# Values projected by pair of groups, and the streams of steps placed anew in one hand-written order

## The reference, cut to what matters

```
xn1 = layernorm(x) * g1 + be1
q, k, v = xn1 @ Wq + bq, xn1 @ Wk + bk, xn1 @ Wv + bv      # per head, 32 wide
scores = (q @ k^T) / scale, masked with -inf above the diagonal
sa  = softmax(scores) @ v
x   = x + sa @ W1 + b1
```

## Time and profile before

| | us |
|---|---|
| median of 3 executions | 2349.78 (2348.75 to 2349.86) |
| span of the profiled execution, first to last instruction | 2338.9 |
| PE busy | 2198.0 (94%) |
| DVE busy | 1410.1 (60%) |
| POOL busy | 933.6 (40%) |
| ACT busy | 868.2 (37%) |
| start of unit 0 / unit 4 / unit 8 / unit 12 | 113.3 / 344.0 / 570.4 / 798.8 |
| start of unit 14 / unit 15 | 898.7 / 965.4 |

### The profile page before, as it was taken

One profiled execution on the slowest core, in us unless ns is written; L12 is line 12 of the kernel. 1 busy time (PEld: TensorE's weight loads), 2 busy tenths in 40 slices (PEclk: granted clock), 3 DMA queues, 4 the chain that ended last, 5 costly groups with the idle time before them and its releaser, 6 DMA issues.

```text
span 2338.9 us, 31417 instructions
## 1 busy us (share of the span) xinstructions
PE 2198.0 (94%) x11206; PEld 1595.5 (68%) x11206; DVE 1410.1 (60%) x3349; ACT 868.2 (37%) x1598; POOL 933.6 (40%) x943
## 2 busy tenths in 40 slices
PE   7999999999999998789999998999999999999996
PEld 5655565556555654447777776788887887888784
DVE  5477757875786566735666668453455546454646
ACT  3155545654565455533443334321111122112213
POOL 1068657766777577773333333010111202011212
PEclk9999999999999998789999999999999999999998
DMA  7465545553556356212111121321112121212011
GB/s 231 55 93 97 92 71 77 103 93 62 83 97 97 60 88 124 69 56 85 59 55 55 59 95 55 113 86 36 50 54 75 52 82 44 87 55 68 33 36 50
DMA packets 106320, 177.29 MB, mean 76 GB/s; under 512 B 18334, under 2 KB 23454, under 8 KB 106160
## 3 DMA queue, kind: packets, MB, share of 16 engines
q1 hardware_dynamic: 106164, 175.29, 32.4%
HBM read 83.67 MB, written 40.13 MB: 53 GB/s over the span
## 4 chain that ended last, share of the span: by engine, by line
PE 75%; DVE 9%; issue 6%; ACT 4%; POOL 3%; DMA 2%; SPq 0%; POOLq 0%; ACTq 0%; DVEq 0%
PE psum L55 18%; PE psum L56 17%; PE psum L57 17%; PE psum L797 5%; PE psum L745 5%; PE psum L785 4%; PE psum L806 2%; DMA small<-es 2%; PE psum L703 1%; DVE psum L1000 1%; POOL es L660 1%; ACT sx L1346 1%; PE psum L1300 1%; DVE mx L1004 1%; PE psum L1292 1%
## 5 line engine op out<-in xcount | busy, mean ns | idle before, releaser
L660 POOL TENSOR_TENSOR es<-es,er 128x512 f32<-128x512 f32 (+3 forms) x640 | 589.6, 961 | 322.5 <-PE psum L797 283.4
L895 ACT ACTIVATE er<-psum 128x512 f32<-128x512 f32 (+3 forms) x640 | 280.4, 470 | 316.0 <-DVE psum L1011 181.2
L1000 DVE CUSTOM_DVE_ANT_0 psum<-psum,mask_ts 128x384 f32<-128x384 f32 (+3 forms) x512 | 247.9, 500 | 201.2 <-PE psum L745 200.5
L785 PE MATMUL psum<-qs,ks 100*128 100x512 f32 (+3 forms) x768 | 264.5, 377 | 17.1 <-DVE mx L1004 6.6
L745 PE MATMUL psum<-ks,qs 96*128 96x512 f32 (+3 forms) x768 | 267.2, 373 | 10.9 <-DVE mx L1000 6.6
L1850 ACT ACTIVATE fy<-psum,cols 128x512 f32<-128x512 f32 x128 | 88.2, 689 | 451.4 <-PE psum L57 450.9
L745 PEld LDWEIGHTS psum<-ks,qs 96*128 96x128 f32 x768 | 144.0, 194 | 109.7 <-issue 39.4
L1004 DVE TENSOR_REDUCE mx<-psum 128x1 fp32r<-128x512 f32 x256 | 175.1, 684 | 60.7 <-PE psum L745 59.8
L785 PEld LDWEIGHTS psum<-qs,ks 100*128 100x128 f32 x768 | 145.9, 196 | 92.4 <-DVE mx L1004 23.1
L55 PE MATMUL psum<-fh,hh 128*128 128x512 f32 x512 | 201.1, 393 | 7.1 <-DVE hl L1951 7.1
L55 PE MATMUL psum<-fah,fh 128*128 128x512 f32 x512 | 202.6, 396 | 0.0
(11 more groups left out here) (258 smaller groups left out, 4479.8 us busy)
## 6 DMA issues: line engine op xcount, KB each, us to landing
qs<-stage SPq DMA_DIRECT2D x96, 256.0 KB, 5.7
ks<-stage SPq DMA_DIRECT2D x96, 256.0 KB, 6.9
rs<-rs_d SPq DMA_DIRECT2D x32, 256.0 KB
sa_d<-rs SPq DMA_DIRECT2D x32, 256.0 KB, 2.2
sx<-sa_d SPq DMA_DIRECT2D x8, 1024.0 KB, 5.7
xt<-in_x SPq DMA_DIRECT2D x32, 256.0 KB, 6.1
x_d<-xt SPq DMA_DIRECT2D x32, 256.0 KB, 2.0
fw<-in_Wf SPq DMA_DIRECT2D x16, 512.0 KB, 5.3
```

The costliest lines, as they stand in the source:

```text
L660: e.tensor_tensor(es, es, er, ALU.add).then_inc(s_add.sem, 1)
L785: t = e.matmul(ps[:, off:512], Q.ks[par][0:100, i, 128 * j:128 * j + 128], Q.qs[par][0:100, i, 512 * c2 + off:512 * c2 + 512], start=True, ...
L895: e.activation(dst, bank1("sc", g, c2, j, i)[:, off:512], ACT.Exp, scale=SCALE).then_inc(s_freeS.sem, 1)
L1000: t = e.tensor_tensor_reduce(out=ps, in0=ps, in1=mask_ts[:, 512 - wd:512], scale=1.0, scalar=-3e38, op0=ALU.add, op1=ALU.max, accum_out=mx ...
```

## The change

1. **Values by pair of groups.** The 8 steps of 512 columns per batch element become 8 steps over two *pairs* q = g // 2 (256 of the 512 columns each): 4 steps `sp` per pair, each of two 128-token blocks. A step has 4 parts, each of 2 k-tiles, so 24 matmuls of 256 columns instead of 12 of 512. One bank and one `ve` (ACT, 512 columns) per step, as before.
2. **`Q.v` becomes a double buffer by pair** (`values(g)`: half g // 2 % 2 of the same memory). `ve` of pair q waits for the last `pv` of group 2q-3, the pair before the last, and for the first two pairs for the `lnT` that read the rows of `x` which lie there at the start.
3. **Positions.** `cut` and the positions of projections, values, row maxima and the normalization now depend on g % 4. Values of the even pair (group g = 4b) stand at g - 1.149, - 0.992, - 0.719, - 0.081; those of the odd pair (group 4b + 2) at g - 1.444, - 1.08, - 0.796, - 0.377. Of group 0 and 1 the maxima are moved ahead.
4. **Cross-attention set-up.** Every position of its first steps is changed a little, the split of `W2` from 15.08 to 15.576, that of `Wq_c` from 14.74 to 14.853, that of `W1` from 14.4 to 14.581; X0 from 16.68 to 16.793.

```
+LN_LOAD = (-2.514, -2.024, -1.712, -1.56)
+LN_TURN = (-2.071, -1.822, -1.573, -1.348)
+CUT = (0.292, 0.27, 0.283, 0.294)
+PROJ_0 = (27.2, 31.3, 37.9, 40.4)
+PROJ_1 = (-1.329, -1.236, -1.109, -1.047)
+PROJ = ((-1.661, -1.491, -1.269, -1.082), (-1.853, -1.456, -1.346, -1.171), (-1.872, -1.647, -1.316, -1.202), (-1.958, -1.475, -1.34, -1.21))
+PROJ_LONG = (0.067, 0.08, 0.146, 0.146)
+VALUES_0 = (40.2, 52.3, 66.7, 68.9)
+VALUES = ((-1.149, -0.992, -0.719, -0.081), (-1.444, -1.08, -0.796, -0.377))
+VALUES_LONG = 0.1
+MAX_0 = -0.007
+MAX_1 = (-0.809, -0.507, -0.024)
+MAX = ((-1.031, -0.726, -0.051), (-1.012, -0.739, -0.002), (-1.033, -0.705, -0.043), (-0.988, -0.72, -0.05))
...
-    cut = 0.31
...
-                t += ln_times(b, qt, 4 * b - 2.5 if qt == 0 else 4 * b - 2.28 + 0.26 * qt, 4 * b - 2.05 + 0.25 * qt)
...
-                s, d = 4 * b - 1 + cut + (1 - cut) * (st + 2.2) / 9, 0.057
+            t += ln_times(b, qt, 4 * b + LN_LOAD[qt], 4 * b + LN_TURN[qt])
...
-        elif g % 4 == 0:
-            at = (g - 1.67, g - 1.5, g - 1.22, g - 1.11)
-        else:
-            at = (max(g - 1.87, 0.2), max(g - 1.63, 0.4), g - 1.4, g - 1.2)
+        at = [at0(a) for a in PROJ_0] if g == 0 else [g + a for a in (PROJ_1 if g == 1 else PROJ[r])]
+        if g % 2 == 0:
+            for sp in range(4):
+                s, d = (at0(VALUES_0[sp]), 0.05) if g == 0 else (g + VALUES[r // 2][sp], VALUES_LONG)
+                t += spread(s, s + d, [(("vm", g // 2, sp, i), 1) for i in range(4)])
+                t.append((s + d, ("ve", g // 2, sp)))
...
-    T, X0 = 0.207, 16.68
+    T, X0 = 0.207, CROSS_AT
-        for j, at in enumerate((14.4, 14.74, 15.08)):
+        for j, at in enumerate(CROSS_SPLIT):
...
+        def values(g):
+            return Q.v[:, 4 * (g // 2 % 2):4 * (g // 2 % 2) + 4, :].rearrange("p a (s n) -> p (a s) n", n=256)
...
-                    t = three(e, bank1(*s[:3]), (Q.xh[:, k, ss], Q.xl[:, k, ss]), (Wh[:, k, :], Wl[:, k, :]), k == 0, k == 3)
+                    for k in range(2 * (i % 2), 2 * (i % 2) + 2):
+                        t = three(e, bank1(*s[:3])[:, to], (Q.xh[:, k, ss], Q.xl[:, k, ss]), (Wh[:, k, cs], Wl[:, k, cs]), k == 0, k == 3)
...
-                    if b:
-                        w.wait_ge(s_pv, Q.pv[4 * b - 1, 1, st, 3] + 1)
+                    if q >= 2:
+                        w.wait_ge(s_pv, Q.pv[2 * q - 3, 1, 2 * sp + 1, 3] + 1)
+                    else:
+                        w.wait_ge(s_fillA, Q.useA["lnT", 0, 2 * q + sp // 2, 1] + 1)
```

More of the change, by code:

```diff
@@ L142, in order1 @@
             t.append((at0(at + 4), ("zo", u)))
[L143 removed]
+    for b in range(1, NB):
         for qt in range(4):
[L145 to L162 removed]
+            t += ln_times(b, qt, 4 * b + LN_LOAD[qt], 4 * b + LN_TURN[qt])
+    for g in range(16):
+        r = g % 4
+        cut = CUT[r]
+        at = [at0(a) for a in PROJ_0] if g == 0 else [g + a for a in (PROJ_1 if g == 1 else PROJ[r])]
         for c2 in range(2):
@@ L165, in order1 @@
                 n = 2 * c2 + wq
[L166 to L169, removed]
+                t += proj_times(g, c2, wq, at[n], at[n] + (0.05 if g < 2 else PROJ_LONG[r]))
@@ new lines, in order1 @@
+                back = g - 2 + (CUT[(g - 2) % 4] if n == 0 else CUT[(g - 2) % 4] + (1 - CUT[(g - 2) % 4]) * 0.54 if n == 1 else 1) + 0.03
+                t.append((at[n] + 0.1 if g == 0 else max(at[n] + PROJ_LONG[r] + 0.07, back), ("stack", g, c2, wq)))
+        if g % 2 == 0:
[3 more added lines that the diff above has]
+                t.append((s + d, ("ve", g // 2, sp)))
@@ L170, in order1 @@
+        m0, m1, end = (at0(46), at0(54), MAX_0) if g == 0 else [g + a for a in (MAX_1 if g == 1 else MAX[r])]
         t += spread(m0, m1, max_steps(g, 0)) + spread(m1, end, max_steps(g, 1))
-        for c2, at in enumerate((m1, end)):
-            t += [(at + 0.04, ("mxT", g, c2)), (at + 0.06, ("tq", g, c2)), (at + 0.09, ("tqd", g, c2))]
+        for c2, a in enumerate((m1, end)):
+            t += [(a + 0.04, ("mxT", g, c2)), (a + 0.06, ("tq", g, c2)), (a + 0.09, ("tqd", g, c2))]
         for c2 in range(2):
-            steps = spread(g + cut * c2, g + (1 if c2 else cut), attn_steps(g, c2))
+            end = g + (1 if c2 else cut)
+            steps = spread(g + cut * c2, end, attn_steps(g, c2))
@@ L175, in order1 @@
             t += steps
-            for at, s in steps:
-                if s[0] == "sc" and s[3] >= 4 * c2:
-                    t += [(at + 0.014, ("low", *s[1:])), (at + 0.028, ("ex", *s[1:]))]
+            for a, s in steps:
+                if s[0] == "sc" and s[3] >= 4 * c2 :
+                    t += [(a + 0.014, ("low", *s[1:])), (a + 0.028, ("ex", *s[1:]))]
                 elif s[0] == "sc":
-                    t.append((at + 0.001, ("ex", *s[1:])))
-            end = g + (1 if c2 else cut)
+                    t.append((a + 0.001, ("ex", *s[1:])))
@@ L240, in order2 @@
         if c == 0:
-            ld, sp, w1, step, ln = 15.78, 15.86, 15.9, 0.07, 16.22
+            (ld, sp, w1, ln), step = CROSS_0, 0.07
         else:
@@ L484, in released @@
             elif use[0] == "vm":
-                w.wait_ge(s_v, 8 * use[1] + use[2] + 1)
+                w.wait_ge(s_v, 4 * use[1] + use[2] + 1)
             elif use[0] == "pj":
```

47 lines of the change are left out of this document (27 added, 20 removed).

## The result

| | before | after |
|---|---|---|
| median | 2349.27 us (4 runs) | 2276.62 us (2275.13 to 2281.93, 4 runs) |
| ratio | | 0.9708, 95% interval 0.9694 to 0.9723 |
| span of the profiled execution | 2338.9 us | 2280.1 us |

The changed kernel is 72.7 us faster; 26 were forecast, and the result lies 20 us under the low end of the range (2297). In this and all sixteen later profiled kernels the execution's own time is known, and it is 1.77 to 1.84 us above the span. So the "10.9 us outside the span" of the prediction was no fixed part: by the same 1.8 us the profiled execution of before took about 2340.7 us, 9 under its median (its own time is not known), and that of after took 2281.93, 5 over its own. The spans therefore show 59 of the 73 us; the other 14 are scatter between executions.

What follows compares the result with a forecast made beforehand. PE, busy 94% of the span, was taken as the bound, so time is won only where it idles or does less work. Terms 2.9 - 14 - 3 - 7 - 3 - 2 = -26 gave 2324 us, range 2297 to 2356.

Steps and rivals of the forecast that it cites:

- 256 columns: Value matmuls on PE: 768 of 256 columns replace 384 of 512, 0.12 us apart; +2.9 us, bounds 0 and +57.
- Rival D: Value matmuls on PE: the weight load sets the pace of 256 columns at 0.19 us; 2378 us, chance 2%.
- Values spread, -14: Attention units: value steps, spread from lumps of 7 and 1, cover PE's waits; -14 us, bounds -28 and +7.
- Double buffer at nothing: `ve` on ACT waits for groups ending over 0.6 of a unit earlier; counted as nothing.
- Projections, maxima, normalization at -3: Small position shifts: POOL stands up to 1.7 us more at `rs`, against better `CUT` shares; -1 per batch element, -3.
- Unit 14 at -7: Unit 14: moved splits shrink the 9.73 us DVE instruction to 1 to 3 us; -7 us, bounds -17 and +17.
- Hand-over at -3: PE's waits entering the next stage: attention's last steps move behind the first wait; -3 us, bounds -11 and +9.
- Clock at -2: Units 5 to 7: value steps nearby remove one or two clock dips of 1.7 us; -2 us, bounds -5 and +3.
- Span to median: Before the first and behind the last instruction: median 10.9 us above the 2338.9 us span, taken as unchanged.
- A: Whole kernel: no change worth the name, steps land where PE is busy anyhow; 2350 us, chance 19%.
- B: Units, normalization, unit 14 and hand-over: all holes filled; 2294 us, chance 15%.
- C: DVE's splits at new places are caught by POOL's adds, up to 8.7 us each; 2360 us with three, chance 12%.

Runs made afterwards that it cites:

- values_only: Changed kernel with every position but the values' set back to those of the kernel before; -34.8 us against the kernel before.
- w1_pool_q_late: Changed kernel with the low part of `W1` made by POOL instead of DVE and the `Wq_c` split at 15.28; 2277.3 us.
- best: `w1_pool_q_late` with the projections of groups 0 and 1 ahead of unit 0 at their old positions; 2274.7 us.
- old_cross: Changed kernel with all positions of the cross-attention's first steps as before; costs 11 us against the changed kernel.
- its control: The changed kernel itself run once more, on the same chip as other experiments; -71.3 us against the kernel before.
- old_ln0: Changed kernel with the normalization and the projections of each batch element's first group at their old positions; 2300.2 us.
- old_lnproj: Changed kernel with normalization and all projections at their old positions; 2320.6 us.
- late_pv: Kernel before with the last `pv` of each half 0.03 of a unit later and its result's copy 0.02 later; 2342.6 us.
- splits_late: Changed kernel with the `W1`, `Wq_c` and `W2` splits later (14.86, 15.28, 15.6) and `W2`'s load at 15.07; 2276.7 us.
- old_max: Changed kernel with the row maxima at their old positions, also those of groups 0 and 1; 2283.6 us.

## Why the prediction was wrong

**The bound on PE.** Right: the time was won in PE's gaps, and the kernel got faster.

**256 columns.** Right: 0.12 us apart, a step at 2.85 to 2.88 us where 2.79 were, some +2 to +3 us in all. Rival D is out. By an estimate from the Trainium skill ("TensorE: Matmul & The Clock Gate", Back-to-back issue gap), whose figures for a stream are 81 ns at 128 columns and 131 ns at 512, two matmuls of 256 would have cost more than one of 512 by at least 31 ns; this trace has 0.24 against 0.233 us, so the row decides.

**Values spread, -14, bounded by -28. This step failed.** It subtracted the value steps from units 4 and 7 and took the remainder, 47.5 us, as what a unit needs. The remainder is the least that was *seen*; units 4 and 7 still lost 7.2 and 7.8 us of it. After the change the same remainder is 45.0 to 45.5 in every unit from 3 to 13 without the normalization's last three quarters, and in `values_only` it is 44.8 to 45.7 in units 7, 11 and 13. The 2.3 us between, times 14 units, are 32 us, and the stretch ahead of unit 14 was forecast to lose 16 us and lost 49. The expected lengths were off by these 2.3 us and by the 0.7 to 1.0 us that the working held back as not covered: 54 for units 5, 9 and 13, measured 50.8, 50.9, 50.7; 57 for units 7 and 11, measured 54.1; unit 4 to unit 8 222, measured 211.0. Net of value steps and transposes, units 4 to 7 became shorter by 1.9, 7.0, 5.0 and 2.3 us, where 0, 2.5, 2.0 and -0.4 were counted; six maxima left unit 5, so part of its 7.0 only moved. By itself the spread gave -35 (`values_only`), beyond its own lower bound.

**Double buffer at nothing.** Not measured by itself; it is a condition of the spread.

**Projections, maxima, normalization at -3. Failed too.** The working looked at one queue, POOL at `rs`, and expected it to stand longer; in unit 6 it stands 2.65 us in place of 5.55, and over the kernel 46.9 in place of 48.8. It also took the new `CUT` as nearer to the first half's real share of a unit, "16.5 of 50". That share is 0.33, and the new 0.27 to 0.29 are farther from it than the old 0.31; in the long units 6 and 7 the same 16 us are 0.27 and 0.25. Set back one at a time, all but the first two groups' projections (0) cost more than the whole term: normalization and first projections 24, other projections 13, `CUT` 24, maxima 7. These costs and the values' 50 are far more than 72 together: they are not shares of the gain. I read each as what it costs when one stream no longer fits the others; by which wait it does stays open. The same new normalization and projections without their partners gave -0.5.

**Unit 14 at -7.** Wrong in place and mechanism. The stall stayed (9.78 us; expected under 4), unit 14 was 64.1 and 60.2 us (expected under 61), and the kernels without the stall (`w1_pool_q_late`, `best`) were no faster. One `Wq_c` split of 4.10 us was caught as well.

**Hand-over at -3.** Measured -5.3 in the traces. The trace of `old_cross` is 5.5 us ahead of the changed kernel's at unit 15's start and loses 9.2 behind it; the two medians are 11 apart.

**Clock at -2.** Half-clock time fell from 27.3 to 6.8 us in the profiles, at most -10; kernels with nearly the same order had 0 to 13.7. In the changed kernel and its control all of it lies in unit 2, in `old_ln0` in units 2, 6 and 10 (6.8 us each), so it adds to what is lost where the normalization runs; in `old_lnproj` unit 0 has 13.7 of the 41.0 us. In the kernel before it was spread over units 1, 2, 6, 9 and 10.

**Span to median.** The 10.9 us "outside the span" are 1.8; that put 9 us of scatter into a constant.

**Rivals.** A did not happen. B, all holes filled, was the nearest in kind, but its 2294 was worked out from the same 47.5 and is 17 us too slow. Of C two instructions were caught (9.78 and 4.10 us) where before it was one.

## What to carry to other kernels

A unit's length net of a filler is an upper bound of what it needs, not the floor: add up its steps at the spacing at which they start back to back, and see what is left. Where all engines go through one hand-written order, price the positions together: parts of such a change can be worth nothing, or half, alone (-0.5 and -35 here), and setting one back can cost more than it had seemed to bring (44). And a wait that is taken away brings less than its length when it opens elsewhere (`late_pv`: 15 us less of it, 5.7 us gained), while the spread of the values around the same steps gave 35.

## What the runs showed of the hardware

Of the DVE splits of `W1`, `Wq_c` and `W2` in the 18 traces, 88 begin while POOL has an add or the product `rs` running. The splits that begin inside a memset of POOL, 17, take their usual 0.63 to 0.74 us.

In 69 of the 88 the split ends 0.55 to 0.63 us after the end of the one POOL instruction then running, and in 3 after the end of the next, though POOL goes on without a break. POOL's next add is the longer one then, for 512 columns 1.7 us in place of 1.27. Two such places, first in the kernel before (DVE, then POOL's next add), then in `values_only` (the same, and POOL's adds around them):

```profile
928.49 1.13 DVE L1392 TENSOR_TENSOR W1l<-raw,W1h 128x512 fp32r<-128x512 f32 x1
...
929.02 1.73 POOL L660 TENSOR_TENSOR es<-es,er 128x512 f32<-128x512 f32 x1
```

```profile
909.41 1.19 DVE L1412 SCALAR_TENSOR_TENSOR Wq_cl<-raw,cols,Wq_ch 128x512 fp32r<-128x512 f32 x1 [0.42 <-ACT Wq_ch L1345]
...
910.00 1.72 POOL L677 TENSOR_TENSOR es<-es,er 128x512 f32<-128x512 f32 x1
...
903.84 19.96 POOL L677 TENSOR_TENSOR es<-es,er 128x512 f32<-128x512 f32 x16
```

In the other 16, in 15 of the traces and all in unit 14, the split takes 4.1 to 10.5 us and ends about 0.55 us after the end of POOL's unbroken run, over 5 to 11 of its instructions. Run ends are at 950.18, 885.51, 893.37, 895.86 and 888.33 us (before, changed, `old_cross`, `splits_late`, `old_max`), DVE's instruction at 950.73, 886.05, 893.92, 896.42 and 888.87. In `splits_late` the run is made of adds of 512 columns, the product `rs` and adds of 256, and DVE stood to the end of the last (893.11 + 2.75).

The Trainium skill ("SBUF — State Buffer", SBUF: two separate sides) says that the one that comes second waits for the other's whole instruction. The 69 agree with that, and so does POOL's longer next add; the 16 show the wait lasting over a whole run. What decides between the two no run shows: both happen in one trace, inside one unbroken run (before, 928.49 and 941.00 us). So the prediction was right that a split can be caught, but a run of POOL's adds around it is not enough for that.
